# A Perceiver layer on one core: for the last six attention units the probabilities are transposed in 32x32 blocks by way of DRAM, and the logits run up to three units ahead in plain float32

## The reference, cut to what matters

```python
xn = layernorm(ctx); ln = layernorm(layernorm(x))
k = rmsnorm((concat[xn, ln] @ Wk).heads);  v = (concat[xn, ln] @ Wv).heads
q = rmsnorm((ln @ Wq).heads) * 64 ** -0.5
out = softmax(q @ k.T) @ v            # 64 x 1088 probabilities a head
x = x + out @ Wout + bout
```

## Time and profile before

| what | value |
|---|---|
| median of 3 runs | 222.93 us (222.92 to 223.26) |
| the profiled execution | 222.66 us, span 220.9 us |
| PE busy | 212.8 us of the span |
| DVE, ACT, POOL busy | 158.5, 148.9, 79.7 us |
| mean granted TensorE clock | 0.999 |

### The profile page before, as it was taken

One profiled execution on the slowest core, in us unless ns is written; L12 is line 12 of the kernel. 1 busy time (PEld: TensorE's weight loads), 2 busy tenths in 40 slices (PEclk: granted clock), 3 DMA queues, 4 the chain that ended last, 5 costly groups with the idle time before them and its releaser, 6 DMA issues.

```text
span 220.9 us, 4126 instructions
## 1 busy us (share of the span) xinstructions
PE 212.8 (96%) x1394; PEld 185.0 (84%) x1394; DVE 158.5 (72%) x362; ACT 148.9 (67%) x329; POOL 79.7 (36%) x129
## 2 busy tenths in 40 slices
PE   6899999999999999999999999999999999999984
PEld 6566878887788898989898889999999997899873
DVE  3889999998968989888878557676877631413531
ACT  4778799979895776858583867876777555315161
POOL 4488887861593846626151300000000010000300
PEclk9999999999999999999999999999999999999999
DMA  6480135200000234152325999720000000000000
GB/s 188 146 307 27 49 119 192 71 27 0 24 3 0 98 97 154 44 185 95 95 95 157 376 397 195 172 48 3 1 0 3 1 0 0 3 0 3 0 0 24
DMA packets 18500, 18.78 MB, mean 85 GB/s; under 512 B 7176, under 2 KB 16560, under 8 KB 18224
## 3 DMA queue, kind: packets, MB, share of 16 engines
q1 hardware_dynamic: 17928, 16.95, 24.5%
q10 hardware_dynamic: 552, 1.58, 2.0%
HBM read 15.51 MB, written 2.75 MB: 83 GB/s over the span
## 4 chain that ended last, share of the span: by engine, by line
PE 69%; DVE 11%; ACT 9%; POOL 5%; issue 5%; POOLq 0%; ACTq 0%; DVEq 0%
PE banks L1440 20%; PE banks L1268 10%; PE banks L1377 9%; PE banks L1337 8%; PE banks L1585 5%; PE banks L1463 4%; PE banks L1470 4%; DVE small L973 3%; DVE sk L985 2%; PE banks L1380 2%; PE banks L1512 2%; PE banks L1612 2%; POOL xn L535 1%; POOL xg L528 1%; ACT knT L687 1%
## 5 line engine op out<-in xcount | busy, mean ns | idle before, releaser
L1016 DVE TENSOR_TENSOR ptl<-banks,pth 128x512 fp32r<-128x512 f32 (+1 forms) x48 | 26.1, 554 | 17.6 <-ACT pth L729 17.3
L1440 PE MATMUL banks<-xnh,pth 128*128 128x256 f32 x128 | 37.6, 294 | 0.0
L1440 PE MATMUL banks<-xnh,ptl 128*128 128x256 f32 x128 | 36.1, 282 | 0.0
L1440 PE MATMUL banks<-xnl,pth 128*128 128x256 f32 x128 | 36.1, 282 | 0.0
L564 POOL TENSOR_TENSOR small<-small 128x16 f32<-128x16 f32 x7 | 20.4, 2915 | 27.3 <-DVE small L980 27.3
L729 ACT ACTIVATE pth<-banks 128x512 fp32r<-128x512 f32 (+1 forms) x48 | 23.7, 494 | 9.5 <-PE banks L1268 8.5
L669 ACT ACTIVATE sk<-banks 128x512 f32<-128x512 f32 x36 | 20.8, 601 | 11.5 <-PE banks L1337 11.0
L973 DVE TENSOR_REDUCE small<-sk 128x8 f32<-128x512 f32 x36 | 23.5, 678 | 3.6 <-ACT sk L669 3.6
L545 POOL COPY sp<-sp 128x64 f32<-128x64 f32 x16 | 4.3, 266 | 59.9 <-ACT sp L708 59.9
L985 DVE TENSOR_TENSOR sk<-banks,small 128x512 f32<-128x512 f32 x36 | 22.9, 679 | 2.7 <-POOL small L564 2.4
L1440 PEld LDWEIGHTS banks<-xnh,pth 128*128 128x128 f32 x128 | 24.4, 191 | 0.5 <-issue 0.4
(11 more groups left out here) (204 smaller groups left out, 474.8 us busy)
## 6 DMA issues: line engine op xcount, KB each, us to landing
knT<-in_L_attn_qkv_kernel SPq DMA_DIRECT2D x1, 3072.0 KB, 12.5
spread<-knT SPq DMA_DIRECT2D x5, 512.0 KB, 2.6
knT<-spread SPq DMA_DIRECT2D x20, 128.0 KB, 2.9
raw<-in_ctx SPq DMA_DIRECT2D x16, 128.0 KB, 2.3
knT<-in_L_xattn_Wq SPq DMA_DIRECT2D x1, 1024.0 KB, 5.7
wv<-in_L_xattn_Wkv ACTq DMA_DIRECT2D x1, 1024.0 KB, 5.9
wout_sb<-in_L_xattn_Wout SPq DMA_DIRECT2D x1, 1024.0 KB, 5.7
knT<-in_L_attn_out_kernel SPq DMA_DIRECT2D x1, 1024.0 KB, 15.9
```

The source lines that it names most:

```text
L1016: nc.vector.tensor_tensor(ptl[:, j0:j1, :], banks[:, t3_bank(u, c), 0:(j1 - j0) * P].rearrange("p (j r) -> p j r", j=j1 - j0), pth[:, j0:j ...
L1440: nc.tensor.matmul(banks[:, u_bank(u), 0:D], p_[:, j, :], x_, start=(j == 0 and i == 0), stop=False)
```

## The change

It does the following.

1. For units 10 to 15 (`SPREAD` = G + 2 = 10) the eight context blocks are no longer transposed on PE. `prob_blocks(u)` on DVE transposes 32x32 blocks of the exponentials into `p_blocks` (one buffer, in `xnh`'s room of batch 0); SP stores it to DRAM, waits for the landing, and loads it back in four DMAs into `p_back` (two buffers). `spread_high` on ACT copies 128x1024 to `pth`, `spread_low` on DVE takes the remainder to `ptl`. The ninth block, the latents, stays with PE (`probs_transposed(u, 2)`).
2. `split_unit` holds only up to unit 10: the logits of units 11 to 15 are plain float32, and their `unit_high` and `unit_low` are gone.
3. The logits of a unit stand up to three units ahead of its mix on PE, and maxima, exponentials and blocks with them on DVE and ACT.
4. `mix(u)` of units 10 to 15 is cut in three: `mix_high` (16 matmuls with pth), `mix_low` (8 with ptl) and `mix_latents` (2); the transposes of the unit before stand between `mix_high(u)` and `mix_low(u)`.
5. SP issues the output kernel after Win1, and Wout2 behind it, ahead of the loop of the blocks; biases and rows follow that loop. The column sums of the output kernel and the transposes of Wout1 and Wout2 move to units 13 and 14 on DVE.

```diff
+            for u in range(SPREAD, UNITS):
+                n = u - SPREAD
+                sp.wait_ge(pb_ready, n + 1)
+                sp.dma_start(p_spread[n], p_blocks).then_inc(pb_stored, 16)
+                sp.wait_ge(pb_stored, 16 * (n + 1))
+                if n >= 2:
+                    sp.wait_ge(ptl_ready, split_count(u - 2, 0))
+                for c in range(4):
+                    sp.dma_start(p_back[n % 2][c * QD:(c + 1) * QD, :].rearrange("a (i m) -> a i m", i=4),
+                                 p_spread[n][:, c * D:(c + 1) * D].rearrange("(i a) m -> a i m", i=4)
+                                 ).then_inc(pq_landed[n % 2], 16)
...
-            return u < UNITS and u % G > 0
+            return u <= SPREAD and u % G > 0
...
+            def spread_high(u):
+                n = u - SPREAD
+                act.wait_ge(pq_landed[n % 2], 64 * (n // 2 + 1))
+                if u == SPREAD:
+                    act.wait_ge(u_ps, u)
+                else:
+                    act.wait_ge(mh_ps, n)
+                    act.wait_ge(ptl_ready, split_count(u - 1, 0))
+                nc.scalar.activation(probs_rows(pth), spread_blocks(p_back[n % 2]), ACT.Copy).then_inc(pth_ready, 1)
...
+            for u in range(SPREAD + 1, UNITS):
+                if u - 2 >= SPREAD:
+                    mixT_out(u - 2)
+                spread_high(u)
+                mix_out(u - 1)
+                if u - 2 >= SPREAD:
+                    heads_out(u - 2)
+                probs_high(u, 2)
+                if u + 3 < UNITS:
+                    exponentials(u + 3)
...
+            def prob_blocks(u):
+                dve.wait_ge(exp_ready, u + 1)
+                if u == SPREAD:
+                    dve.wait_ge(u_ps, G)
+                else:
+                    dve.wait_ge(pb_stored, 16 * (u - SPREAD))
+                nc.vector.transpose(p_blocks.rearrange("p (j c r) -> p c j r", j=4, r=QD),
+                                    sp2[:, u % 2, 0:J].rearrange("p (c j r) -> p c j r", c=NT, r=QD)).then_inc(pb_ready, 1)
...
+            for u in range(SPREAD + 1, UNITS):
+                mix_low(u - 1)
+                mix_latents(u - 1)
+                if u - 2 >= SPREAD:
+                    values(u - 2)
+                if u + 1 < UNITS:
+                    probs_transposed(u + 1, 2)
+                if u + 3 < UNITS:
+                    all_logits(u + 3)
```

More of the change, by code:

```diff
@@ L403, in t3_bank @@
                 return 1
+            if u >= G and c == 2:
+                return 2 if u < SPREAD else (0, 6)[u % 2]
             return 0 if c != 1 or u < G else 6
@@ L832, in _ @@
             squares(ITEMS_A + 1, 1)
-            for u in range(UNITS):
+            for u in range(G - 1):
                 i = ITEMS_A + u
@@ L1512, in attended, with all_logits @@
                 return nc.tensor.matmul(banks[:, 2, 0:D], oT[:, g, :], wout_sb[:, g, :], start=(g == 0), stop=(g == G - 1))
-            for u in range(UNITS - 1):
+            def all_logits(u):
+                for part in range(3):
+                    logits(u, part)
+            for u in range(G):
                 i = ITEMS_A + u
@@ L1517, in _ @@
                     probs_transposed(0, 0)
-                    for part in range(3):
-                        logits(1, part)
+                    all_logits(1)
                     probs_transposed(0, 1)
@@ L1528, in _ @@
                     mix_transposed(u - 1)
-                    if i < ITEMS and i not in BLOCKED:
+                    if i not in BLOCKED:
                         keys_transposed(i, 0)
@@ L1540, in _ @@
                         project(i + 1, 1)
-                    if u < G:
-                        logits(u + 1, 0)
-                        logits(u + 1, 1)
+                    logits(u + 1, 0)
+                    logits(u + 1, 1)
                     probs_transposed(u, 2)
-                if u > 0:
                     logits(u + 1, 2)
-                mix(u)
-                if u > G + 1:
-                    attended(u - G - 2)
+                if u < G - 1:
+                    mix(u)
+            mix(G - 1, (0, 1))
@@ new lines, in _ @@
+            all_logits(G + 1)
+            mix(G - 1, (2,))
+            for c in range(3):
+                probs_transposed(G, c)
+            mix_transposed(G - 1)
+            all_logits(G + 2)
+            values(G - 1)
+            mix(G)
+            for c in range(3):
+                probs_transposed(G + 1, c)
+            mix_transposed(G)
+            all_logits(G + 3)
+            values(G)
+            mix(G + 1, (0,))
+            probs_transposed(G + 2, 2)
+            all_logits(G + 4)
@@ new lines, in _ @@
+            mix(G + 1, (1, 2))
+            probs_transposed(G + 3, 2)
+            mix_transposed(G + 1)
+            all_logits(G + 5)
+            values(G + 1)
+            mix_high(SPREAD)
+            for u in range(SPREAD + 1, UNITS):
+                mix_low(u - 1)
[4 more added lines that the diff above has]
+                    probs_transposed(u + 1, 2)
+                if u + 3 < UNITS:
+                    all_logits(u + 3)
+                for g in range(2 * (u - UNITS + 3), min(2 * (u - UNITS + 3) + 2, 5)):
+                    if g >= 0:
+                        attended(g)
+                if u == UNITS - 1:
+                    pe.wait_ge(xb_ready, 1)
+                    nc.tensor.matmul(banks[:, 2, 0:D], ident[:, :], xb[:, :], start=False, stop=False)
+                    mix_transposed(u - 1)
+                mix_high(u)
+                if u < UNITS - 1:
+                    mix_transposed(u - 1)
@@ L1551, in _ @@
             u = UNITS - 1
-            probs_transposed(u, 0)
-            probs_transposed(u, 1)
-            mix_transposed(u - 1)
+            values(u - 1)
             attended(G - 3)
-            pe.wait_ge(xb_ready, 1)
-            nc.tensor.matmul(banks[:, 2, 0:D], ident[:, :], xb[:, :], start=False, stop=False)
-            mix(u, (0,))
-            values(u - 1)
-            probs_transposed(u, 2)
-            mix(u, (1,))
+            mix_low(u)
             attended(G - 2)
-            mix(u, (2,))
+            mix_latents(u)
```

194 lines of the change are left out of this document (149 added, 45 removed).

## The result

The changed kernel takes 224.48 us, the median of 17 runs (223.37 to 226.62), against 223.13 (222.69 to 224.47) for the kernel before in the same comparison: ratio 1.006, 95% interval 1.0041 to 1.0079. It is 0.6% slower, 1.35 us, where 222.9 us and no change were forecast, and it lies 0.2 us above the forecast's range of 220.9 to 224.3.

The account below looks back on a forecast made before the run. The prediction took PE as the bound. Work of -2.7, the wait at `values(10)` +1.7, smaller waits +1.45 and -0.2 at unit 15 gave +0.25 on 222.66: 222.9 us, no change, range 220.9 to 224.3.

Parts of the forecast that it names:

- PE's own work: PE, units 9 to 15: transposes -4.2, logits +1.25 and -0.15, mix in two pieces +0.4, together -2.7 us.
- +0.7 behind `mix(9)`: PE behind `mix(9)`: only one transpose left to fill ACT's copy of the finished sum, a wait of 0.7 us.
- +0.25 ahead of unit 10's logits: PE ahead of unit 10's logits: they wait 0.25 us for unit 9's maximum.
- Five units: +1.25: PE's logits of units 11 to 15: plain at 1.81 us instead of split at 1.56, +1.25 us.
- The wait at `values(10)`: PE ready at T + 9.2, ACT's copy at T + 10.9, through `prob_blocks(13)` waiting for unit 12's store: 1.7 us.
- Rival 4: DVE's list is longer in every unit and paces two to three units: about +1 us, 223.9; chance 0.12.
- rival 2: At `values(10)`, the wait for unit 12's store is hidden: -1.7 us, 221.0; chance 0.2.
- The DMA's price is known here: Stores of the blocks: five earlier stores of this size landed in 2.6 us, so these take 2.64.
- I put its cost at nothing: Unit 10's first trip: last load lands about 148.4, ACT asks at 149.2; thin cover of 0.8 us, no cost.
- rival 3: Unit 10's first blocks land late behind the output kernel's 1 MB, ACT stands in `spread_high(10)`: 224.1 us; chance 0.18.
- Later units have 2 us or more: Trips of the units after unit 10: their landings have 2 us or more of cover.
- 0.35 + 0.15 for `heads_out` behind a large copy: PE at `mix_high(13)` and `mix_high(15)`: waits of 0.35 and 0.15 us for `heads_out`, behind a large copy on ACT.

Follow-up runs that it names:

- the run with the output kernel early: The changed kernel with the output kernel's load moved back right behind the qkv load, the rest as changed: 223.57 us.
- the run with the lows first: The changed kernel with DVE's block transpose of unit 13 moved behind unit 11's low parts and unit 14's maximum: 224.50 us.
- two buffers with ACT's order: The changed kernel with two block buffers, `heads_out(u-2)` ahead of `mix_out(u-1)` on ACT, and at unit 15 `mix_out(14)` ahead of `spread_high(15)`: 223.33 us.

## Why the prediction was wrong

**PE's own work: right in kind, 0.85 us too small.** For the new order without the trip the prediction has -2.7, -0.2 at unit 15, +0.7 behind `mix(9)` and +0.25 ahead of unit 10's logits: -1.95. Without the trip the stretch shrank by 56.21 - 53.38 = 2.8. The two waits came to size: less what the transposes ahead of them take, they are 149.78 - 149.05 - 0.11 = 0.62 behind `mix(9)` (the forecast's own terms add up to 0.63, not 0.7), at unit 10's logits 135.05 - 134.56 - 0.22 = 0.27. The logits' term, "Five units: +1.25", was mis-sized: it should have been 5 x 0.16 = 0.8. I took it from unit 8's row; the same instructions cost 0.16 or 0.34 a unit more than the split ones, by what stands ahead of them. And a term was missing: the two transposes of a finished sum, now between `mix_high` and `mix_low`, take 159.64 - 159.50 = 0.14 for 0.22 before, five times. That is the other 0.4.

**The wait at `values(10)`: right.** From T, the end of unit 13's logits and start of `values(9)`, I had PE ready at T + 9.2 and the copy there at T + 10.9. In the run with the output kernel early T is 151.80, PE is ready at 160.88 + 0.12 = T + 9.2, and `values(10)` starts at 162.70 = T + 10.9. In the changed kernel (T = 153.48, where `values(9)` starts, 0.3 behind the logits) the same wait of 1.7 stands 0.65 later: PE is ready at T + 9.85 and `values(10)` starts at 165.03 = T + 11.55. Unit 10's loads were late, `spread_low(10)` with them, and DVE's whole list behind it: `prob_blocks(13)` starts at T + 6.1, not T + 5.2. Unit 12's store took 2.67 for 2.64, `spread_low` 1.21 for 1.22, `spread_high` 1.06 for 1.05. The run with the lows first shows that the cause is the one named. Rival 4 is out with these durations; so is rival 2, for the wait is there.

**"The DMA's price is known here": the step that failed.** 2.64 us holds where no DMA has just been issued ahead, and only unit 12's store, the one that I worked through, had that. The trace of before had no store right behind loads: its keys' tiles are a unit apart. Here the stores of units 11 and 13 to 15 go out as soon as the loads ahead of them are issued, and land in 3.4 to 3.7, and unit 10's, behind the tail's weights, in 5.3; the run that waits for the landings has 2.7 from unit 11 on. What this cost is shown for unit 10 alone (next); for the later units no run separates it.

**"I put its cost at nothing": the second step that failed.** Ahead of unit 10 the landing exceeded its cover: the store took 5.3 us for 2.6, and ACT stood for 1.13 us (0.62 in the trace with an ordinary first stretch). That is rival 3, with the idle of ACT ahead of the first copy out of `xnh_room` that was named as its sign, at a cost of 0.9 by the run with the output kernel early. It was named with the right place and a chance of 0.18.

**"Later units have 2 us or more": the third step that failed.** I followed the chain for unit 13 only, and took the rest from the lead of three units. A trip is a block transpose, a store and four loads: unit 15's store goes out at 173.11, the loads at 176.62, and ACT has them at 182.29, 1.72 after it asks; for unit 11 it waits 0.65. PE then waits 1.11 for `mix_out(14)`, which stands behind `spread_high(15)` in ACT's list. The prediction had 0.15 at unit 15. The order of ACT's copies, worth 1.4 us beside the run with two buffers alone, is about these waits.

**The sum.** All waits of the trip are 224.48 - 220.36 = 4.1 us. I had 1.7, and 0.35 + 0.15 for `heads_out` behind a large copy, which without the trip are gone too: 2.2. With the work of -2.7 by the same medians, 1.4 us of loss. So I had the waits 1.9 us too small and the gain 0.75 us too small, and it is luck that the second hides part of the first. What the runs take back of the waits: 0.9 by the output kernel, 1.15 by two buffers with ACT's order (2.0 together), perhaps 0.4 at unit 15. The 1.7 to 2.1 left above the run without a trip I take for the trip's length where three units of lead don't cover it; no run separates them. What quicker stores would give, on another engine's queue for one, wasn't tried. Nor did any run keep one buffer and change ACT's order alone.

## What to carry to other kernels

To take work off the busy engine is worth only what the new path's latency leaves. Time a kernel that has the new order without the trip, and one that makes the trip for nobody: two runs gave the ceiling (-2.7 us), the waits (4.1) and the traffic's cost (none). Then look at the order on the engine in between: a copy that somebody waits for must not stand behind one that waits for a DMA, and a buffer that is added without that moves the wait and wins nothing. A DMA's landing time from a queue on which nothing has just been issued is not its time in a loop.

## What the runs showed of the hardware that I had not expected

- A store of 512 KB takes 2.67 us to land where the last DMA of its queue was issued 1.9 us before, though that one is still in flight (unit 12); 3.3 to 3.8 where it is issued right behind four loads of 128 KB. One store of the first kind took 3.07 (unit 12 with the lows first); why stays open.
- Right behind the output kernel's 1 MB and Wout2's four loads of small pieces it takes 5.1 to 5.5 us in five traces (4.4 in the one whose trip is unread), without that 1 MB 2.9 to 3.3 in four.
- Doubling the DMA engines' share in 54 us (0.29 to 0.63, 78 to 192 GB/s) left the second stretch at 53.38 us.
- The plain float32 logits take 1.72 us a unit in one run. In halves with four transposes ahead of each it is the same 0.86 a half, but the transposes' group takes 0.44 instead of 0.35.
